# A two-layer relational graph convolution on one Trainium2 core: node numbers read from PSUM, both octs of a block aggregated before its products, four banks added in one go

## What is computed

```python
def _rgcn_layer(x, src, dst, edge_type, w_rel, root, bias):
    N = x.shape[0]
    seg = dst * NUM_REL + edge_type
    xs = x[src]
    sums = jax.ops.segment_sum(xs, seg, num_segments=N * NUM_REL)
    cnt = jax.ops.segment_sum(jnp.ones(seg.shape, x.dtype), seg, num_segments=N * NUM_REL)
    mean = (sums / jnp.maximum(cnt, 1.0)[:, None]).reshape(N, NUM_REL, -1)
    return jnp.einsum('nrd,rdo->no', mean, w_rel) + x @ root + bias
...
edge_type = jnp.argmax(msg[:, NODE_EMB_DIM:-NODE_EMB_DIM], axis=1).astype(jnp.int32)
h = jax.nn.relu(_rgcn_layer(x, src, dst, edge_type, w_rel1, root1, b1))
return _rgcn_layer(h, src, dst, edge_type, w_rel2, root2, b2)
...
x = _layernorm(x + _L0_gnn_ref(x, ...), axis=-1)
```

## Time and profile before

| | |
|---|---|
| median of 3 runs | 4248.94 us |
| lowest and highest | 4235.66, 4250.05 us |
| the profiled execution, its own time | 4252.87 us |
| its span, first to last instruction | 4251.2 us |
| busy PE, PEld, DVE, ACT, POOL | 2114.3, 1993.4, 2271.6, 961.9, 3229.2 us |
| gathers (POOL, L1305) | 3126 |
| mean granted clock of TensorE | 0.729 of full |

### The profile page before, as it was taken

The page is one execution under the profiler, slowest core; times in us unless marked ns, Lnnn a source line. Parts: engine busy times, 40 slices in busy tenths (PEclk is TensorE's granted clock), DMA queues, the critical chain, the costliest instruction groups (busy, mean ns, idle before and its releaser), DMA issues.

```text
span 4251.2 us, 55995 instructions
## 1 busy us (share of the span) xinstructions
PE 2114.3 (50%) x12375; PEld 1993.4 (47%) x12376; DVE 2271.6 (53%) x5257; ACT 961.9 (23%) x3133; POOL 3229.2 (76%) x3140
## 2 busy tenths in 40 slices
PE   2544555445444555555545554445545555555554
PEld 2544444444444444444434444444444444444444
DVE  7766666666666666666634444444444444444444
ACT  1222222222222222222212222222222222222222
POOL 7777777777777777777757777777777777777775
PEclk6777777777777777777777777777777677777777
DMA  5222222222222222222212222222222222222221
GB/s 112 72 71 70 71 71 71 68 71 70 71 71 71 72 72 71 71 71 64 53 46 59 62 59 59 59 59 60 59 58 59 60 59 59 59 59 62 57 60 45
DMA packets 206602, 275.41 MB, mean 65 GB/s; under 512 B 62732, under 2 KB 156428, under 8 KB 206444
## 3 DMA queue, kind: packets, MB, share of 16 engines
q0 software_dynamic: 100032, 205.07, 18.4%
q1 hardware_dynamic: 101534, 67.96, 5.7%
q10 hardware_dynamic: 4878, 0.86, 0.2%
HBM read 260.85 MB, written 12.80 MB: 64 GB/s over the span
## 4 chain that ended last, share of the span: by engine, by line
POOL 66%; issue 22%; PE 6%; DVE 3%; DMA 2%; ACT 0%; POOLq 0%; DVEq 0%; ACTq 0%; SPq 0%
POOL rows L1305 66%; PE ps_agg L1603 4%; DVE z_s L1899 1%; PE ps_agg L1599 1%; DMA rows<-in_x_dram,idx_s 1%; DMA rows<-table,idx_s 1%; DVE S L1816 1%; PE ps_y L1622 1%; ACT prod L1504 0%; DVE ring L1863 0%; DVE cnt_ring L1836 0%; POOLq L1327 0%; PE ps_agg L1580 0%; POOLq L1329 0%; ACT idx_s L1466 0%
## 5 line engine op out<-in xcount | busy, mean ns | idle before, releaser
L1305 POOL DMA_INDIRECT rows<-table,idx_s x1563 | 1577.3, 1009 | 506.5 <-issue 472.6
L1305 POOL DMA_INDIRECT rows<-in_x_dram,idx_s x1507 | 1583.5, 1051 | 459.5 <-issue 454.4
L1603 PE MATMUL ps_agg<-S,rows 128*128 128x140 f32 x6272 | 1356.0, 384 | 0.0
L1603 PEld LDWEIGHTS ps_agg<-S,rows 128*128 128x128 f32 x6272 | 1319.2, 283 | 36.4 <-issue 0.2
L1863 DVE TENSOR_TENSOR ring<-ps_agg,ring 128x440 f32 x784 | 483.7, 617 | 1174.2 <-PE ps_agg L1603 1162.8
L1599 PE MATMUL ps_agg<-zero_b 128*128 128x440 bf16 x784 | 379.5, 484 | 1016.9 <-DMA rows<-table,idx_s 818.6
L1836 DVE TENSOR_TENSOR cnt_ring<-ps_agg,cnt_ring 10x14 f32 x1568 | 264.3, 169 | 665.9 <-PE ps_agg L1603 587.2
L1599 PEld LDWEIGHTS ps_agg<-zero_b 128*128 128x128 bf16 x784 | 110.9, 141 | 1070.1 <-issue 1044.5
L1580 PE MATMUL ps_agg<-hit,hit_typ 128*128 128x56 bf16 x392 | 83.9, 214 | 1011.5 <-DMA rows<-in_x_dram,idx_s 878.3
L1899 DVE TENSOR_REDUCE z_s<-prod 128x128 f32<-128x1536 f32 (+1 forms) x196 | 563.8, 2876 | 6.0 <-ACT prod L1509 5.5
L1466 ACT COPY idx_s<-idx_t 128x8 uint32 (+1 forms) x385 | 75.9, 197 | 2165.3 <-PE ps_agg L1603 2165.3
(11 more groups left out here) (114 smaller groups left out, 969.5 us busy)
## 6 DMA issues: line engine op xcount, KB each, us to landing
attr<-in_edge_attr_dram SPq DMA_DIRECT2D x97, 336.0 KB, 3.0
rows<-table,idx_s POOLq DMA_INDIRECT x1563
rows<-in_x_dram,idx_s POOLq DMA_INDIRECT x1507
x_in<-in_x_dram SPq DMA_DIRECT2D x97, 64.0 KB, 1.9
table<-h_s SPq DMA_DIRECT2D x97, 64.0 KB
x_in<-table SPq DMA_DIRECT2D x97, 64.0 KB, 1.9
prod<-in_x_dram SPq DMA_DIRECT2D x97, 64.0 KB
out_dram<-o_s SPq DMA_DIRECT2D x97, 64.0 KB
```

The lines of the kernel that those rows point to most:

```text
L1305: pool.indirect_dma_start(out=rows[:, slot, j, :], out_offset=None, in_=(x, htab)[l][:, :], in_offset=bass.IndirectOffsetOnAxis(ap=at, axi ...
L1603: ins = t_.matmul(bank[:, bass.ds(off[j] * R, TCOL)], lhsT=rows[:, o % PER, j, :], rhs=S[:, o % PER, j, :], start=False, stop=(c == 3))
```

## The change

1. **Node numbers in PSUM.** `iota_p`, 140 columns of ps_misc, gets a copy of iota_c once; make_S reads iota_p. The first two types are taken before the first hits and S.
2. **Order within a step.** VectorE makes hits and S of both octs, then the types, in layer 1 then normalises block s - 4 (before: s - 3 at the end), waits for ring_zeroed, adds four banks, and only then gives the reciprocals and adds up z_s. TensorE aggregates both octs and then transforms. ScalarE copies both octs' indices before it finishes block s - 3.
3. **Types in a quad's bank.** TensorE turns the types of step s + 2 within the step's second oct, into columns RCOL of the first quad's bank, and VectorE takes them from there. typ_a has three buffers.

```diff
-        typ_a = sb("typ_a", [P, 2, P], BF16)
+        typ_a = sb("typ_a", [P, 3, 2, P], BF16)
+        typ_place = [0, 1, 0, 1, 0, 1, 2]
...
+        iota_p = ps_misc[:, 320:320 + TCOL]
...
                             next_indices(l, i, 2 * k, last)
+                            next_indices(l, i, 2 * k + 1, last)
                             if not (first and k < 3):
                                 finish(l, s - 3)
-                            next_indices(l, i, 2 * k + 1, last)
...
-                def turn_types(s):
+                def turn_types(s, k, bank, at):
 
                     pe.wait_ge(typ_ready, s + 1)
                     for h in range(2):
-                        ins = t_.matmul(ps_misc[:, h * GT:(h + 1) * GT], lhsT=typ_a[:, h, :], rhs=pick[:, :],
-                                        start=True, stop=True)
-                    ins.then_inc(typ_turned, 1)
+                        ins = t_.matmul(bank[:, at + h * GT:at + (h + 1) * GT], lhsT=typ_a[:, typ_place[k], h, :],
+                                        rhs=pick[:, :], start=True, stop=True)
+                    return ins
...
+                            if h == 0 and typ is not None:
+                                turn_types(*typ, bank, RCOL)
...
-                            if l == 0 and not (last and k >= PER - 2):
-                                pe.wait_ge(typ_taken, s + 2)
-                                turn_types(s + 2)
...
                             aggregate(l, i, 2 * k, off, last, ((k - 2) % PER, s * 4 - 2) if behind else None)
+                            off = offsets(i * (2 * PER) + 2 * k + 1)
+                            types = (s + 2, (k + 2) % PER) if l == 0 and not (last and k >= PER - 2) else None
+                            aggregate(l, i, 2 * k + 1, off, last, typ=types)
                             if behind:
                                 transform(l, s - 2, (k - 2) % PER, s * 4 - 2,
                                           (i if k > 0 else i - 1) * 16 + (l * LAPS * 16 + 16))
-                            off = offsets(i * (2 * PER) + 2 * k + 1)
-                            aggregate(l, i, 2 * k + 1, off, last)
...
-                    v_.tensor_tensor(S[:, sl, :, :], bc1(iota_c[:, :], GT, TCOL),
+                    v_.tensor_tensor(S[:, sl, :, :], bc1(iota_p, GT, TCOL),
                                      bc(comb_t[:, bass.ds(g * GT, GT)], GT, TCOL), ALU.is_equal).then_inc(S_ready, 1)
...
-                take_types(0)
+                dve.wait_ge(typ_turned, 1)
+                take_types(0, ps_misc[:, 0:2 * GT])
                 make_types(2, 0, 2, 16)
-                dve.wait_ge(typ_taken, 1)
+                dve.wait_ge(typ_turned, 2)
+                take_types(1, ps_misc[:, 0:2 * GT])
+                link(v_.tensor_copy(iota_p, iota_c[:, :]))
                 for o in range(2):
                     make_hits(o, o)
                     make_S(o, o)
-                take_types(1)
...
-                                if h == 0:
-                                    dve.wait_ge(ring_zeroed, s + (l * NBLOCK + 1))
-                                add_oct(l, i, o, s - 2 if h == 0 and not (first and k < 2) else None, k)
-                                if h == 0:
-                                    if not (first and k < 2):
-                                        give_reciprocals(l, s - 2)
...
-                                    if not (first and k < 3):
-                                        add_up(l, s - 3)
-                            if l == 1 and not (first and k < 3):
-                                normalise(s - 3)
+                            if l == 0 and not (last and k >= PER - 3):
+                                ahead, full = (k + 3) % PER, (k + 3) // PER
+                                tail = isinstance(i, int) and i * PER + k + 3 == NBLOCK - 1
+                                make_types(s + 3, None, ahead, (i + full) * 16 + (32 if tail else 16))
+                            if l == 1 and not (first and k < 4):
+                                normalise(s - 4)
+                            dve.wait_ge(ring_zeroed, s + (l * NBLOCK + 1))
+                            add_oct(l, i, 2 * k, s - 2 if not (first and k < 2) else None, k)
+                            add_oct(l, i, 2 * k + 1, None, k,
+                                    s + 2 if l == 0 and not (last and k >= PER - 2) else None)
+                            if not (first and k < 2):
+                                give_reciprocals(l, s - 2)
+                            if not (first and k < 3):
+                                add_up(l, s - 3)
+                    if l == 1:
+                        normalise(NBLOCK - 4)
```

More of the change, by code:

```diff
@@ L1583, in count, with aggregate @@
                               start=True, stop=True)
-                def aggregate(l, i, o, off, last, rc=None):
+                def aggregate(l, i, o, off, last, rc=None, typ=None):
                     g = i * (2 * PER) + (l * OCTS + o)
@@ L1630, in _ @@
                     if l == 0:
-                        turn_types(0)
+                        turn_types(0, 0, ps_misc, 0).then_inc(typ_turned, 1)
                         pe.wait_ge(typ_taken, 1)
-                        turn_types(1)
+                        turn_types(1, 1, ps_misc, 0).then_inc(typ_turned, 1)
                     else:
@@ L1789, in make_types, with take_types @@
                     dve.wait_ge(typ_step, s * 3 + 3)
-                    if not (isinstance(s, int) and s == 0):
-                        dve.wait_ge(typ_turned, s)
+                    if isinstance(s, int) and s == 2:
+                        dve.wait_ge(typ_turned, 1)
                     for h in range(2):
                         t8 = typ_p[:, h * GT:(h + 1) * GT].rearrange("p (u j) -> p u j", u=1).to_broadcast([P, 16, GT])
-                        ins = v_.scalar_tensor_tensor(out=typ_a[:, h, :].rearrange("p (a j) -> p a j", j=GT), in0=t8,
+                        ins = v_.scalar_tensor_tensor(out=typ_a[:, typ_place[k], h, :].rearrange("p (a j) -> p a j", j=GT), in0=t8,
                                                       scalar=-float(R), in1=spread[:, :, :], op0=ALU.add, op1=ALU.mult)
                     ins.then_inc(typ_ready, 1)
-                def take_types(s):
+                def take_types(s, turned):
                     cols = bass.ds(s * (2 * GT), 2 * GT)
-                    dve.wait_ge(typ_turned, s + 1)
-                    v_.tensor_copy(typ_t[:, cols], ps_misc[:, 0:2 * GT])
-                    v_.scalar_tensor_tensor(out=comb_t[:, cols], in0=rel_t[:, cols], scalar=float(R),
-                                            in1=ps_misc[:, 0:2 * GT], op0=ALU.mult, op1=ALU.add
-                                            ).then_inc(typ_taken, 1)
+                    v_.tensor_copy(typ_t[:, cols], turned)
+                    v_.scalar_tensor_tensor(out=comb_t[:, cols], in0=rel_t[:, cols], scalar=float(R), in1=turned,
+                                            op0=ALU.mult, op1=ALU.add).then_inc(typ_taken, 1)
                 def make_hits(g, sl):
@@ L1847, in take_counts, with add_oct @@
                     v_.tensor_copy(rc_all[:, bass.ds(b * R, R)], rc_t[:, :]).then_inc(rc_step, 1)
-                def add_oct(l, i, o, behind, k):
+                def add_oct(l, i, o, behind, k, types=None):
                     g = i * (2 * PER) + o
@@ L1861, in add_oct @@
                                 take_counts(behind, (k - 2) % PER, bank[:, RCOL:RCOL + R])
+                            if h == 0 and types is not None:
+                                take_types(types, bank[:, RCOL:RCOL + 2 * GT])
                         win = ring[:, :, bass.ds(pos[h], QWIN)]
@@ L1941, in _ @@
                                 dve.wait_ge(typ_taken, s + 2 if not (last and k == PER - 1) else NBLOCK)
-                                if not (last and k >= PER - 2):
-                                    take_types(s + 2)
                             for h in range(2):
```

4 lines of the change are left out of this document (removed).

## The result

| | before | after |
|---|---|---|
| median of 3 runs | 4248.94 us | 3991.19 us |
| lowest and highest | 4235.66, 4250.05 | 3991.19, 3991.71 |
| span of the profiled execution | 4251.2 us | 3989.5 us |
| busy time of the 3126 gathers | 3225.4 us | 2961.1 us |
| mean granted clock of TensorE | 0.729 | 0.753 |

The ratio is 0.9403, with a 95% interval of 0.9374 to 0.9431. The forecast was 4008 us.

The account below looks back on a forecast made before the run. The prediction took GpSimd's line of gathers, lengthened by VectorE's S, as the bound. From 4252.9 us, less 258.3 for S, plus 13 for small instructions and 4 at the ends, less 3.9, it forecast 4008 us, range 3985 to 4085.

Parts of the forecast that it names:

- What bounds the kernel: GpSimd never stops for data, row buffers or indices: 3126 gathers at 0.947 + 0.305 us, plus 265.1 us of lengthening.
- Part 1: VectorE's make_S with node numbers in PSUM no longer holds gathers: all 258.3 us go; S's own length costed at nothing.
- Part 2: Layer 0's hit, hit_typ, two ahit and typ_a keep two SBUF inputs and lengthen gathers: about 13 us added.
- the prediction's own formula: Average loss to a gather starting evenly in a 1.25 us period: (length - 0.13) squared / 2.5.
- bound below: For the small instructions in layer 0: 0 at best if the phase is nearly the same in every block; 98 us at worst.
- Part 3: Four banks in one go, transform behind both octs, types in a quad's bank: 0 in steady state, +4 us at the ends.
- The base of the sum: Profiled execution of 4252.9 us as starting point, and 3.9 us off because the timed runs' median lay below it.
- Rival (a): Small VectorE instructions take S's place in holding gathers, adding 30 to 85 us: 4040 to 4095 us; chance 7%.
- Rival (b): S still holds gathers through its length or SBUF output; back-to-back order leaves 163 of 258 us: 4158 us; chance 9%.
- Rival (c): Reading a 140-column PSUM row eight times over is slow and VectorE becomes the bound: 4390 us; chance 2%.
- Rival (d): S is freed but GpSimd's 0.305 us pause grows or it waits elsewhere, 240 us in all: 4249 us; chance 3%.

Follow-up runs that it names:

- node numbers alone: Kernel after with the order of work put back as before, node numbers in PSUM and types in a quad's bank kept: 3984.71 us; 4902.63 us on a slower chip.
- order alone: Kernel after with make_S reading iota_c in SBUF again, order and types as after: 4135.22 us; 4945.85 us on a slower chip.
- exchanged: Kernel after with S's operands swapped, comb_t from SBUF first and node numbers from PSUM second: 4977.93 us, ratio 1.042, on a slower chip.
- tail variant: Kernel after with reciprocals and z_s ahead of the second oct's adds in each layer's last step: 5062.30 us, ratio 1.051, on a slower chip.
- eight variants: The first eight follow-up kernels, each an edit of the kernel after, run on two slower chips: ratios to before there 1.026 to 1.080.
- last four kernels: Later runs on another chip: the kernel after unchanged, and three of the earlier edits of it again: 3990.98, 4135.22, 3984.71 and 3980.37 us.
- one more from SBUF: Kernel after with an extra S-like instruction in each step, both inputs in SBUF, output never read: 5036.78 us, ratio 1.050, on a slower chip.
- small ones and tail: Kernel after with small instructions' constants in PSUM and z_s ahead of the last oct's adds: 3980.37 us; 5084.21 us on a slower chip.

## Why the prediction was right, point by point

The time came out at 3991.19, inside the range and 16.8 below the 4008. By its steps:

- **What bounds the kernel**: right. GpSimd is a line of 3126 gathers and pauses before and after, and the span fell by what the gathers' busy time fell.
- **Part 1, -258.3 us for S**: right in mechanism and size. 343 held gathers became none, and the gathers under ring adds, on which I had argued, foretold it. (253 of them start with at least 0.16 us of the add left, which the prediction doesn't say; 403 start inside an add at all, and none takes over 0.962 us.) S itself costs the same from PSUM, 1316 against 1321 ns. The prediction's reading of this, that the ring add lies within 10 ns of S's rate, doesn't follow from its two lengths, since a line can be drawn through any two; only the run settles it. The rule of the Trainium skill, SBUF — State Buffer, section Who interferes with whom, that a VectorE instruction with two SBUF inputs contends with a GpSimd instruction that reads SBUF, agrees with the held gathers here. The sentence further down there, marked as inferred, by which `tensor_tensor` would leave descriptor generation alone, doesn't hold for an indirect gather: the extra instruction from SBUF held 139 of them. No run here has a GpSimd transfer without indices.
- **Part 2, +13 us for the small instructions**: wrong in size; it is +0.6. The steps that failed are "a gather starting evenly at any time in a period" and the pair hit, hit_typ taken as one piece of 0.42 us. A gather is pushed over 1.0 us if more than 1.0 - 0.82 = 0.18 us is left of what holds it. Evenly, 196 x 0.24 / 1.25 = some 38 gathers would start that early in a pair; in after it is 19 (84 start in a pair at all, mostly late in it), and of these only 8 take over 1.0 us. Of the other eleven, four start within 0.01 us of the start of hit and aren't held. Seven show that the pair isn't one piece: four are let go at the end of hit (one with 0.182 us of hit and 0.335 us of the pair left takes 1.000 us), and three that start 0.08 to 0.12 us before hit's end aren't held at all. Costed one by one, by the prediction's own formula, hit and hit_typ come to an estimated 2.3 us instead of 6.6. The total came out near the prediction's bound below, "0 at best". The same instructions in PSUM save 3 us of lengthening, which bounds what they cost. Putting the small costs evenly over time had been tested on S, which is longer than a gather's period and meets one whatever the phase; that says nothing of instructions a third as long.
- **Part 3, nothing in the steady state, +4 at the ends**: right to a microsecond. GpSimd's waits for idx_s are 4.9 us in all, as against 8.9 before. The tail cost 2.0 where I had 2.8, the border 1.2 where I had 1. The order's price measured against node numbers alone is 2.8 in the tail, 1.5 at the border and 3.3 in the gathers, 7.6 of the 8.0 between the two spans.
- **The base of the sum**: two small things were wrong in it, and they carry it from 4008 to 3991 together with Part 2. The gathers that nobody holds take 0.9438 instead of 0.9459 us on average, 6.6 us in all. It isn't the operand: the mean is 0.944 in the order-alone run that keeps S in SBUF and about 0.946 in the traces of the exchanged and the tail variant, which have it in PSUM. What it is stays open. And the profiled execution of after lies at the median of its runs, while I took 3.9 us off for before. 12.4 of Part 2, 6.6 of the gathers' base, 0.6 at the ends and 0.8 of pauses, less the 3.9, make 16.5 of the 16.8.
- **Rival (a)**, small instructions at 40 us or more: fallen, as above.
- **Rival (b)**, S still holds gathers by length or output: fallen by 0 of 341. But its arithmetic, the value of the back-to-back order while S does hold gathers, could be tested with the order alone: it gave 163 us of holding and 4158 us; measured were 147.5 and 4135.22. The second S of a pair holds gathers in layer 0 only (some 32 of the 100.6 us there), as it said, and layer 0 comes out near its 98 x 0.98 = 96 us. The miss is in layer 1: 46.8 us against its 98 x 0.68 = 67, where it had carried over the mean of 0.66 us for each S of the kernel before.
- **Rival (c)**, slow reads of 140 columns eight times over: fallen, 1316 ns. Its slack was a little too large: a layer-0 block took 16 x (1.051 + 0.305) = 21.7 us, not 20.9, so VectorE needed 13.9 us of it, not 13.3. Nothing hung on that. **Rival (d)**: fallen, the pause is unchanged at 0.305.

## What to carry to other kernels

Where one engine works in a steady beat, take its shortest instruction as the price and ask of each longer one which other engine's instruction it ends behind, at a constant distance; that points to the partner and to what about it matters. If a VectorE instruction that reads two SBUF inputs meets indirect gathers, put its constant operand in PSUM before reordering anything: here the operand was worth 258 us alone, the order 108 alone and nothing beside it. (The types' product was moved out of that bank for it; no run shows what sharing the bank would do.) Look first whether the gathers set the pace where the kernel runs: on two of the chips here they didn't, and none of the eight variants was faster than before there. And an instruction shorter than the beat should be costed by itself and with its phase in the trace, not as if it fell evenly.

## What the hardware showed that I had not expected

- **The same code had another bound on other chips.** Before took 4249 us beside the first timing of after and 4243 twice beside the last four kernels, but 4778 and 4825 beside the first eight. In the eight traces from there 741 to 990 of VectorE's queue instructions take 0.6 us or more each, where the same line takes 67 ns elsewhere, and the mean granted clock of TensorE is 0.66 to 0.67 instead of 0.72 to 0.75. On such a chip none of the eight variants was faster than before (1.026 to 1.080). The kernel after was not among them; the nearest to it, the order alone and the exchanged operands, were 3.5 and 4.2% slower. The cause is open.
- **A held gather is released by the end of the instruction, not shared with it.** In the four traces with such an instruction (before, order alone twice, one more from SBUF) it ends 0.811 to 0.833 us behind that end, whether it started 0.015 or 1.135 us into it (the ends of the 343 in before). The instruction has to read both inputs from SBUF; one input in PSUM is enough to free it, in 965 gathers that start under such an instruction, with at least 0.16 us of it left, in four kernels (341, 253, 237, 134).
- **The instruction can be the one that gives way.** In before, 11 gathers that start in the first 0.042 us of an S aren't held at all (0.947 or 0.948 us). It is S that is longer there: 1.361 to 1.399 us instead of 1.319, and it ends 1.356 to 1.358 us behind the start of the gather in each case. The other three traces have 11 more of the kind. The 190 S of before that start 0.05 us or more into a gather take at most 1.328 us, so what the two share is taken by the gather only for a moment near its start.
- **The beat of an unheld gather has two levels**, a mean of 0.944 and one of 0.946 us, by nothing that I can name; over 3126 gathers that is 7 us. Each kernel that was traced twice (after, order alone, node numbers alone, small ones and tail) was at 0.944 both times, although the last three of these ran on two chips each; before, exchanged and tail, traced once each, were at 0.946. So it may belong to the code and not to the execution.
